# Head of a fused normalisation, attention and gated-MLP kernel: statistics and roots by two tiles, first product in column halves, first down weights split earlier

## The chip, the cores and the metric

The kernel runs on one core of a Trainium2 chip. The metric is the device time of one execution in microseconds. An execution of the kernel before takes 474.47 us (median of 3 runs, 474.45 to 474.83).

## What is computed

The input x has 2048 tokens of 512 features, in fp32. It is normalised over its features; the result feeds an attention over the 32 heads of each token by itself (query 16 by 32, key and value 16 by 8, each used for four heads) and a gated MLP with 1792 inner features. The MLP's result goes through a SiLU and gates the attention's result, and x is added.

```python
x = L0_attn_x                                    # (1, 2048, 512)
xn = _layernorm(x, axis=-1)
# attention of xn: q, k, v = xn @ W + b; scores over the 16 x 16 of one token
scores = jnp.einsum('bsdh,bseh->bsde', q, k) / np.float32(np.sqrt(D))
attn = jax.nn.softmax(scores, axis=-1)
out = jnp.einsum('bsde,bseh->bsdh', attn, v)
# MLP of xn
var = jnp.mean(jnp.square(x), axis=-1, keepdims=True)
nx = x * jax.lax.rsqrt(var + RMS_EPS) * ln_w
g = jnp.einsum('bsh,ih->bsi', nx, gate_w)
u = jnp.einsum('bsh,ih->bsi', nx, up_w)
return jnp.einsum('bsi,hi->bsh', jax.nn.silu(g) * u, down_w)
# end
g = _silu(_L0_ffn_ref(xn, ...))
x = x + s * g
```

## The kernel before

**Tiles.** A tile is 128 tokens by 512 features; four tiles (J) make a block of 512 tokens (TB), two blocks a pair (JJ = 8 tiles), and there are two pairs. Block 0 of the first pair is tiles 0 to 3, block 1 is tiles 4 to 7. The 1792 inner features are 14 groups (NI) of 128. Each operand of TensorE is kept as a high part (rounded to the matmul's format) and a low part (the rest), and each product is three matmuls: high by high, low weights by high data, high weights by low data. From group 1 on the gate and up products of two blocks are done by a scheme of seven products instead of eight (m1 to m7); group 0 is "plain": gate and up of block 0, then of block 1.

**Order.** Nothing is scheduled by the machine. Each engine has one queue written out by hand, and semaphores tie them. Five queues matter in the head, the first 28 us:

- SP issues the loads, in this order: x tiles 0 to 3, lnw, gate 0, the two halves of wq, up 0, wk, wv, x tile 4, the three biases, x tiles 5 to 7, gate 1, up 1 and two down weights.
- DVE (VectorE) takes the statistics of a tile (stats_tile, L1075), its mean and variance (variance, L1059 and L1061), and for tiles 0 to 3 normalises it (normalise_tile, L1070). Then it makes the low parts of the first weights (first_lo, L1166), four tiles of z_lo (L1119), the rest of first_lo, the statistics of tiles 4 to 7 with the low parts of the qkv weights (lo_qkv, L1289) behind those of tile 4, and takes the qkv products out of PSUM (qkv_take, L1192).
- POOL (GpSimd) takes the roots: scale_tile (L477, and for tiles 4 to 7 the shift, L482) and rms_of (L486, L487, L489), which qkv_take needs. It sums the queries' weights over four heads (sum_queries, L511 and L514) and the query bias (L526, L529), and later makes low parts: wd_lo_part (L504) and h_lo_part (L498).
- ACT (ScalarE) makes high parts: first_hi (L807), z_hi_tile (L840), hi_qkv (L953), hi_wd (L828), h_hi_part (L916). It normalises tiles 4 to 7 (z_tile, L833) and copies transposed tiles to SBUF (z_raw_tile, L844).
- TensorE (PE) runs 32 warm-up transposes, transposes tiles 0 to 3 (L727), and then first_gate0 (L583, L586, L589), first_up0 (L599, L600, L603), qkv_product(0) (L714, L715, L718), tile 4's transposes, qkv_product(1), the transposes of tiles 5 and 6, qkv_product(2), tile 7, qkv_product(3), gate1 and up1 of group 0 (L572 to L574), four more qkv products, and from there the groups 1 to 13 (L553, L555, L556 and the down products, L687 to L689).

A tile of block 1 is transposed into the PSUM bank (y_ps) of the tile four before it, once z_raw_tile has copied that one. The order of ACT in the middle of the head is z_tile(4), z_tile(5), z_hi_tile(4), z_tile(6), z_tile(7), z_raw_tile(4), z_hi_tile(5), z_hi_tile(6). In the code J is 4, so L833 for tile 5 is z_tile(J + 1).

## Time and profile before

| | |
|---|---|
| median of 3 runs | 474.47 us |
| the profiled execution's own time | 474.35 us |
| its span, first to last instruction | 472.6 us |
| around the span | 1.75 us |
| TensorE busy | 466.3 us, 99% |
| DVE busy | 412.7 us, 87% |
| ACT busy | 244.2 us, 52% |
| POOL busy | 123.1 us, 26% |
| DMA | 105.70 MB, mean 224 GB/s |

A busy share counts the time in which an engine executes; a row of the timeline gives the start, the duration, the engine, the line and the tiles of one instruction, or of several merged ones (xN). Starts are microseconds from the span's start. PEld is TensorE's loading of weights, which overlaps its matmuls (PE). SPq is the queue of SP as it issues DMAs.

### The profile page before, as it was taken

Reading aid. Unit: us, or ns where it says so; the run is one execution under the profiler, and the core shown is the slowest. Engines: PE = TensorE matmul, PEld = TensorE weight load, DVE = VectorE, ACT = ScalarE, POOL = GpSimd, SP = SyncE. Lnnn points to the kernel's source line nnn. Section 1 sums busy time; section 2 is a strip of 40 time slices with the busy share of each in tenths; the row PEclk is TensorE's granted clock in tenths of the full one; section 3 lists DMA queues with packets and bytes.
Section 4 is the critical chain, followed back from the end, with each engine's and each line's share of the span. In section 5 each row is a group of like instructions: output and inputs, shape, how many; then the busy total and the mean of one; then the engine's idle time right before and its main releaser. Section 6 shows DMA issues by size and latency. Waiting matters only on the chain.

```text
span 472.6 us, 6217 instructions
## 1 busy us (share of the span) xinstructions
PE 466.3 (99%) x2122; PEld 391.0 (83%) x2122; DVE 412.7 (87%) x561; ACT 244.2 (52%) x417; POOL 123.1 (26%) x106
## 2 busy tenths in 40 slices
PE   7999999999999999999999999999999999999997
PEld 7898888888888888888888888888888888888886
DVE  6889778987898898889989898999998888888994
ACT  4785656658588888654122545225225335358102
POOL 5740312126222122233443101000011111126920
PEclk9999999999999999999999999999999999999999
DMA  8605996579779996573474649546556655514772
GB/s 269 252 2 225 345 380 262 234 259 273 205 248 301 298 360 255 188 268 133 135 235 162 218 187 371 202 184 223 222 201 223 223 200 200 201 44 135 276 259 89
DMA packets 44623, 105.70 MB, mean 224 GB/s; under 512 B 20272, under 2 KB 21808, under 8 KB 41264
## 3 DMA queue, kind: packets, MB, share of 16 engines
q1 hardware_dynamic: 44592, 105.31, 63.3%
q8 instruction: 17, 0.28, 0.2%
q14 instruction: 14, 0.11, 0.1%
HBM read 69.90 MB, written 35.40 MB: 223 GB/s over the span
## 4 chain that ended last, share of the span: by engine, by line
PE 95%; DVE 2%; DMA 1%; ACT 1%; SPq 0%; POOL 0%; issue 0%
PE gu_ps L553 18%; PE gu_ps L555 18%; PE gu_ps L556 18%; PE y_ps L687 8%; PE y_ps L688 8%; PE y_ps L689 8%; PE gu_ps L688 3%; PE gu_ps L687 3%; PE gu_ps L689 3%; PE gu_ps L718 2%; PE gu_ps L715 2%; PE gu_ps L714 2%; DMA xz<-x 1%; DVE w_ops L1166 1%; PE y_ps L727 0%; DVE stats L1075 0%
## 5 line engine op out<-in xcount | busy, mean ns | idle before, releaser
L553 PE MATMUL gu_ps<-z_hi,w_ops 128*128 128x512 f32 x378 | 147.2, 390 | 0.1
L556 PE MATMUL gu_ps<-z_hi,w_ops 128*128 128x512 f32 x378 | 147.1, 389 | 0.0
L555 PE MATMUL gu_ps<-z_lo,w_ops 128*128 128x512 f32 x378 | 147.1, 389 | 0.0
L498 POOL TENSOR_TENSOR h_lo<-h,h_hi 128x512 fp32r<-128x512 f32 x28 | 37.4, 1335 | 226.8 <-ACT h_hi L916 226.6
L553 PEld LDWEIGHTS gu_ps<-z_hi,w_ops 128*128 128x128 f32 x378 | 71.0, 188 | 15.5 <-issue 0.4
L556 PEld LDWEIGHTS gu_ps<-z_hi,w_ops 128*128 128x128 f32 x378 | 70.9, 188 | 14.8
L555 PEld LDWEIGHTS gu_ps<-z_lo,w_ops 128*128 128x128 f32 x378 | 70.9, 188 | 14.5
L687 PE MATMUL y_ps<-wd_ops,h_hi 128*128 128x512 f32 x168 | 65.6, 390 | 0.0
L689 PE MATMUL y_ps<-wd_ops,h_lo 128*128 128x512 f32 x168 | 65.5, 390 | 0.0
L688 PE MATMUL y_ps<-wd_ops,h_hi 128*128 128x512 f32 x168 | 65.5, 390 | 0.0
L916 ACT ACTIVATE h_hi<-h 128x512 fp32r<-128x512 f32 x28 | 17.6, 630 | 58.9 <-DVE h L1208 58.9
L1250 DVE TENSOR_TENSOR prod<-scores,qkv 128x1024 f32<-128x1024 f32 x32 | 43.2, 1351 | 0.8
L1232 DVE TENSOR_TENSOR prod<-qkv 128x1024 f32<-128x1024 f32 x32 | 41.8, 1305 | 0.6
L1253 DVE TENSOR_REDUCE attn<-prod 128x64 f32<-128x1024 f32 x32 | 38.9, 1217 | 0.8
L1235 DVE TENSOR_REDUCE scores<-prod 128x128 f32<-128x1024 f32 x32 | 38.9, 1215 | 0.6
L687 PEld LDWEIGHTS y_ps<-wd_ops,h_hi 128*128 128x128 f32 x168 | 31.5, 188 | 6.9 <-POOL h_lo L498 0.6
L689 PEld LDWEIGHTS y_ps<-wd_ops,h_lo 128*128 128x128 f32 x168 | 31.5, 188 | 6.6
L688 PEld LDWEIGHTS y_ps<-wd_ops,h_hi 128*128 128x128 f32 x168 | 31.5, 188 | 6.3
L891 ACT ACTIVATE u<-gu_ps 128x512 f32<-128x512 f32 x27 | 16.1, 598 | 38.9 <-PE gu_ps L556 38.9
L504 POOL TENSOR_TENSOR wd_ops<-raw,wd_ops 128x512 fp32r<-128x512 f32 x14 | 19.7, 1405 | 57.4 <-ACT wd_ops L828 27.6
L1220 DVE TENSOR_TENSOR h_kept<-u 128x512 f32<-128x512 f32 x27 | 22.3, 828 | 12.8 <-ACT u L904 10.0
L498 POOL TENSOR_TENSOR h_lo<-h_kept,h_hi 128x512 fp32r<-128x512 f32 x15 | 23.3, 1556 | 35.4 <-ACT h_hi L916 34.4
(139 smaller groups left out, 753.0 us busy)
## 6 DMA issues: line engine op xcount, KB each, us to landing
w_kept<-w_ops SPq DMA_DIRECT2D x13, 1792.0 KB, 6.2
w_ops<-w_kept SPq DMA_DIRECT2D x13, 1792.0 KB, 7.6
wd_ops<-wd_kept SPq DMA_DIRECT2D x35, 512.0 KB, 4.0
raw<-gate_up SPq DMA_DIRECT2D x30, 256.0 KB, 3.9
wd_kept<-wd_ops SPq DMA_DIRECT2D x14, 512.0 KB, 7.8
xz<-x SPq DMA_DIRECT2D x16, 256.0 KB, 5.3
raw<-down SPq DMA_DIRECT2D x14, 256.0 KB, 8.5
w_ops<-wd_kept SPq DMA_DIRECT2D x7, 512.0 KB, 7.5
```

The costliest lines, as they stand in the source:

```text
L498: pool.tensor_tensor(lo, src, hi.bitcast(F32), ALU.subtract).then_inc(h_lo_done, 1)
L553: pe.matmul(acc, w_h, z_hi[:, zi, c, :], start=start and c == 0, stop=False, skip_group_check=True)
L555: pe.matmul(acc, w_h, z_lo[:, zi, c, :], start=False, stop=False, skip_group_check=True)
L556: end = pe.matmul(acc, w_l, z_hi[:, zi, c, :], start=False, stop=c == 1, skip_group_check=True)
L687: pe.matmul(acc, hi, wd[:, 0, t], start=n == 0, stop=False, skip_group_check=part)
L688: pe.matmul(acc, hi, wd[:, 1, t], start=False, stop=False, skip_group_check=part)
L689: pe.matmul(acc, lo, wd[:, 0, t], start=False, stop=n == NI - 1, skip_group_check=part)\
L1220: dve.tensor_tensor(h_kept[:, g % NI, :], u2[:], up, ALU.mult).then_inc(h1_done, 1)
L1232: return dve.tensor_tensor(pr, q[:, d:d + HALF, :].unsqueeze(2).to_broadcast([P, HALF, D, HKV]), k.unsqueeze(1).to_broadcast([P, HALF, D, ...
L1235: return dve.tensor_reduce(s[:, d:d + HALF, :], pr, X, ALU.add)
L1250: return dve.tensor_tensor(pr, e[:, d:d + HALF, :].unsqueeze(2).to_broadcast([P, HALF, HKV, D]), v.unsqueeze(1).to_broadcast([P, HALF, HKV ...
L1253: return dve.tensor_reduce(o[:, d:d + HALF, :], pr, X, ALU.add)
```

## The change

- lnw is loaded by ACT's queue instead of SP's, ahead of its table load. On SP's queue up 0 goes ahead of wq, and x tiles 5 and 6 ahead of the biases.
- DVE takes the statistics of tiles 0 and 1, then the variance of both in one instruction, then the same for 2 and 3, and only then normalises the four tiles. POOL takes the roots of two tiles in one instruction (scale_two). x_variance(0) stands behind first_lo(0).
- On POOL rms_of for tiles 0 to 3 goes from ahead of sum_queries to behind scale_tile(J), which is tile 4's root and shift.
- TensorE's first_gate0 and first_up0 become first_products: the gate's products of high parts and those with z_lo are made in two halves of 256 columns, each waiting for its own two tiles, and a part of the up products stands between the two halves with z_lo. qkv_product(0) waits for wqkv by halves.
- On ACT first_hi(1) goes ahead of the first two z_raw_tile, and hi_wd(0) from behind the last z_raw_tile to between z_hi_tile(J + 2) and z_raw_tile(J + 1).

```diff
@@ -400,19 +400,18 @@
                         sp.dma_start(out_tiles[J * f + j, :, t], fin_x[f][:, j, t]).then_inc(fin_stored, 16)
 
             load_x(0, range(0, J))
-            sp.dma_start(lnw_sb[:], lnw).then_inc(lnw_in, 16)
             load_gate(0)
+            load_up(0)
             for a in (0, 2):
                 sp.dma_start(wq_raw[:, a:a + 2, :], wq.rearrange("(k p) n -> p k n", p=P)[:, a:a + 2, :])\
                   .then_inc(wq_in[a // 2], 16)
-            load_up(0)
             sp.dma_start(wqkv_raw[:, :, DG:2 * DG], wk.rearrange("(k p) n -> p k n", p=P)).then_inc(wkv_in, 16)
             sp.dma_start(wqkv_raw[:, :, 2 * DG:], wv.rearrange("(k p) n -> p k n", p=P)).then_inc(wkv_in, 16)
-            load_x(0, (J,))
+            load_x(0, range(J, JJ - 1))
             sp.dma_start(bq_raw, bq.partition_broadcast(P)).then_inc(bias_in, 16)
             sp.dma_start(bias[:, DG:2 * DG], bk.partition_broadcast(P)).then_inc(bias_in, 16)
             sp.dma_start(bias[:, 2 * DG:], bv.partition_broadcast(P)).then_inc(bias_in, 16)
-            load_x(0, range(J + 1, JJ))
+            load_x(0, (JJ - 1,))
             load_gate(1)
             load_up(1)
             load_down(0)
@@ -471,15 +470,18 @@
                                pattern=[[-1, P]], channel_multiplier=1).then_inc(const_done, 1)
             pool.wait_ge(const_done, 3)
 
+            def scale_two(j):
+                pool.wait_ge(var_done, j + 2)
+                t = slice(j, j + 2)
+                pool.tensor_tensor(z_scale[:, t], z_var[:, t], minus_half[:, t], ALU.pow).then_inc(z_scale_done, 2)
+
             def scale_tile(j):
-                pool.wait_ge(var_done, j + 1 + (j >= J))
-                t = slice(j, j + 1)
+                pool.wait_ge(var_done, j + 2)
+                t, m = slice(j, j + 1), slice(j - J, j - J + 1)
                 pool.tensor_tensor(z_scale[:, t], z_var[:, t], minus_half[:, t], ALU.pow).then_inc(z_scale_done, 1)
-                if j >= J:
-                    m = slice(j - J, j - J + 1)
-                    pool.wait_ge(z_scale_done, j + 1)
-                    pool.wait_ge(mean_done, j - J + 1)
-                    pool.tensor_tensor(z_shift[:, m], minus_mean[:, m], z_scale[:, t], ALU.mult).then_inc(z_shift_done, 1)
+                pool.wait_ge(z_scale_done, j + 1)
+                pool.wait_ge(mean_done, j - J + 1)
+                pool.tensor_tensor(z_shift[:, m], minus_mean[:, m], z_scale[:, t], ALU.mult).then_inc(z_shift_done, 1)
 
             def rms_of(first, count, step, tile):
                 t = slice(first, first + count)
@@ -514,13 +516,13 @@
                 pool.tensor_tensor(wqkv_raw[:, k, 0:DG], quads[:, :, :, 0, 0], quads[:, :, :, 1, 0], ALU.add)\
                     .then_inc(wqkv_summed, 1)
 
-            for j in range(J):
-                scale_tile(j)
-            pool.wait_ge(var_done, J + 1)
-            rms_of(0, J, 1, 0)
+            scale_two(0)
+            scale_two(2)
             sum_queries(0)
             sum_queries(1)
             scale_tile(J)
+            pool.wait_ge(var_done, J + 1)
+            rms_of(0, J, 1, 0)
             pool.wait_ge(bias_in, 48)
             bias_quads = bq_raw.rearrange("p (n s r) -> p n s r", s=2, r=2)
             pool.tensor_tensor(bias_quads[:, :, :, 0], bias_quads[:, :, :, 0], bias_quads[:, :, :, 1], ALU.add)\
@@ -574,34 +576,42 @@
                         end = pe.matmul(acc, w_l, z_hi[:, zi, c, :], start=False, stop=last)
                 return end
 
-            def first_gate0():
-                acc = gu_ps[:, GATE_BANK, :]
-                chunks = [(wi, zi, c) for wi, zi in ((WA11, ZB11), (WA12, ZB21)) for c in range(2)]
+            def first_products():
+
+                gate, up = gu_ps[:, GATE_BANK, :], gu_ps[:, UP_BANK, :]
+                gates = [(wi, zi, c) for wi, zi in ((WA11, ZB11), (WA12, ZB21)) for c in range(2)]
+                ups = [(wi, zi, c) for wi, zi in ((WA21, ZB11), (WA22, ZB21)) for c in range(2)]
+                halves = slice(0, TB // 2), slice(TB // 2, TB)
+
+                def w_part(s, wi, c):
+                    return w_ops[:, 0, s, wi, c * P:(c + 1) * P]
+
                 pe.wait_ge(w_hi_a, 1)
-                pe.wait_ge(z_hi_done, J)
-                for n, (wi, zi, c) in enumerate(chunks):
-                    pe.matmul(acc, w_ops[:, 0, 0, wi, c * P:(c + 1) * P], z_hi[:, zi, c, :], start=n == 0, stop=False)
+                for a, t in enumerate(halves):
+                    pe.wait_ge(z_hi_done, 2 * a + 2)
+                    for n, (wi, zi, c) in enumerate(gates):
+                        pe.matmul(gate[:, t], w_part(0, wi, c), z_hi[:, zi, c, t], start=a + n == 0, stop=False,
+                                  skip_group_check=True)
                 pe.wait_ge(w_lo_a, 1)
-                for wi, zi, c in chunks:
-                    pe.matmul(acc, w_ops[:, 0, 1, wi, c * P:(c + 1) * P], z_hi[:, zi, c, :], start=False, stop=False)
+                for wi, zi, c in gates:
+                    pe.matmul(gate, w_part(1, wi, c), z_hi[:, zi, c, :], start=False, stop=False, skip_group_check=True)
+                pe.wait_ge(z_lo_done, 2)
+                for wi, zi, c in gates:
+                    pe.matmul(gate[:, halves[0]], w_part(0, wi, c), z_lo[:, zi, c, halves[0]], start=False, stop=False,
+                              skip_group_check=True)
+                pe.wait_ge(w_hi_a, 2)
+                for n, (wi, zi, c) in enumerate(ups):
+                    pe.matmul(up, w_part(0, wi, c), z_hi[:, zi, c, :], start=n == 0, stop=False)
                 pe.wait_ge(z_lo_done, J)
-                for n, (wi, zi, c) in enumerate(chunks):
-                    end = pe.matmul(acc, w_ops[:, 0, 0, wi, c * P:(c + 1) * P], z_lo[:, zi, c, :], start=False,
-                                    stop=n == 3)
+                for n, (wi, zi, c) in enumerate(gates):
+                    end = pe.matmul(gate[:, halves[1]], w_part(0, wi, c), z_lo[:, zi, c, halves[1]], start=False,
+                                    stop=n == 3, skip_group_check=True)
                 end.then_inc(m2_done, 1)
-
-            def first_up0():
-                acc = gu_ps[:, UP_BANK, :]
-                chunks = [(wi, zi, c) for wi, zi in ((WA21, ZB11), (WA22, ZB21)) for c in range(2)]
-                pe.wait_ge(w_hi_a, 2)
-                for n, (wi, zi, c) in enumerate(chunks):
-                    w_h = w_ops[:, 0, 0, wi, c * P:(c + 1) * P]
-                    pe.matmul(acc, w_h, z_hi[:, zi, c, :], start=n == 0, stop=False)
-                    pe.matmul(acc, w_h, z_lo[:, zi, c, :], start=False, stop=False)
+                for wi, zi, c in ups:
+                    pe.matmul(up, w_part(0, wi, c), z_lo[:, zi, c, :], start=False, stop=False)
                 pe.wait_ge(w_lo_a, 2)
-                for n, (wi, zi, c) in enumerate(chunks):
-                    end = pe.matmul(acc, w_ops[:, 0, 1, wi, c * P:(c + 1) * P], z_hi[:, zi, c, :], start=False,
-                                    stop=n == 3)
+                for n, (wi, zi, c) in enumerate(ups):
+                    end = pe.matmul(up, w_part(1, wi, c), z_hi[:, zi, c, :], start=False, stop=n == 3)
                 end.then_inc(m4_done, 1)
 
             def gate1(g):
@@ -709,12 +719,14 @@
                 zi, t = 2 * (j // J), slice((j % J) * P, (j % J + 1) * P)
                 z_h = [z_hi[:, zi + k // 2, k % 2, t] for k in range(K)]
                 z_l = [z_lo[:, zi + k // 2, k % 2, t] for k in range(K)]
-                pe.wait_ge(wqkv_hi_done, 2)
                 for k in range(K):
+                    if index == 0:
+                        pe.wait_ge(wqkv_hi_done, k // 2 + 1)
                     pe.matmul(acc, z_h[k], wqkv_hi[:, k, :], start=k == 0, stop=False)
                     pe.matmul(acc, z_l[k], wqkv_hi[:, k, :], start=False, stop=False)
-                pe.wait_ge(wqkv_lo_done, 2)
                 for k in range(K):
+                    if index == 0:
+                        pe.wait_ge(wqkv_lo_done, k // 2 + 1)
                     end = pe.matmul(acc, z_h[k], wqkv_lo[:, k, :], start=False, stop=k == K - 1)
                 end.then_inc(qkv_done, 1)
 
@@ -736,8 +748,7 @@
                 pe.transpose(y_ps[:, 0, 0:P], ident[:], ident[:])
             for j in range(J):
                 transpose_tile(y_ps[:, j, :], j)
-            first_gate0()
-            first_up0()
+            first_products()
             qkv_product(0)
             second_tile(J)
             qkv_product(1)
@@ -944,6 +955,7 @@
                     acc = gu_ps[:, j, t] if f == 3 and n == 0 else y_ps[:, j, t]
                     act.activation(fin_y[:, j, t], acc, ACT.Silu).then_inc(y_done, 1)
 
+            act.dma_start(lnw_sb[:], lnw).then_inc(lnw_in, 16)
             load_silu()
             act.wait_ge(lnw_in, 16)
             def hi_qkv(half_of_k):
@@ -955,9 +967,9 @@
             first_hi(0)
             for j in range(J):
                 z_hi_tile(j)
+            first_hi(1)
             z_raw_tile(0)
             z_raw_tile(1)
-            first_hi(1)
             hi_qkv(0)
             hi_qkv(1)
             z_raw_tile(2)
@@ -971,11 +983,11 @@
             z_raw_tile(J)
             z_hi_tile(J + 1)
             z_hi_tile(J + 2)
+            hi_wd(0)
             z_raw_tile(J + 1)
             z_hi_tile(J + 3)
             z_raw_tile(J + 2)
             z_raw_tile(J + 3)
-            hi_wd(0)
             h_hi_part(0)
             scale(1)
             hi_a(1)
@@ -1054,9 +1066,16 @@
 
         @block.vector
         def _(dve):
-            def variance(j):
+            def aggregate(j):
                 dve.wait_ge(bn_done, j + 1)
                 dve.bn_aggr(mean_var[:, j, :], stats[:, j, :]).then_inc(stats_done, 1)
+
+            def two_variances(j):
+                dve.wait_ge(stats_done, j + 2)
+                dve.tensor_scalar(z_var[:, j:j + 2], mean_var[:, j:j + 2, 1], 1.0 + EPS, EPS * EPS,
+                                  ALU.mult, ALU.add).then_inc(var_done, 2)
+
+            def variance(j):
                 dve.wait_ge(stats_done, j + 1)
                 dve.tensor_scalar(z_var[:, j:j + 1], mean_var[:, j, 1:2], 1.0 + EPS, EPS * EPS,
                                   ALU.mult, ALU.add).then_inc(var_done, 1)
@@ -1290,22 +1309,22 @@
                                   ALU.subtract).then_inc(wqkv_lo_done, 1)
 
             dve.memset(scratch[:, 0:1], 0.0).then_inc(table_loaded, 1)
+            for j in (0, 2):
+                stats_tile(j)
+                stats_tile(j + 1)
+                aggregate(j)
+                aggregate(j + 1)
+                two_variances(j)
             for j in range(J):
-                stats_tile(j)
-                if j:
-                    variance(j - 1)
-                if j > 1:
-                    normalise_tile(j - 2)
-            variance(J - 1)
-            normalise_tile(J - 2)
+                normalise_tile(j)
+            first_lo(0)
             x_variance(0)
-            normalise_tile(J - 1)
-            first_lo(0)
             for j in range(J):
                 z_lo_tile(j)
             first_lo(1)
             for j in range(J, JJ):
                 stats_tile(j)
+                aggregate(j)
                 variance(j)
                 mean_of(j)
                 if j == J:
```

## Rows read from the trace of the kernel before

**Rows 1.** Page, 40 slices of the span: granted clock of TensorE, tenths

```profile
PEclk9999999999999999999999999999999999999999
```

**Rows 2.** Waits of TensorE, whole span: us in total, times, longest

```profile
PE gu_ps L583 <- ACT z_hi L840: 0.8, 1, 0.8
```

**Rows 3.** Waits of TensorE's weight loads, 27 us to the end

```profile
PEld gu_ps L553 <- issue: 0.4, 1, 0.4
PEld gu_ps L553 <- ACT u L891: 0.3, 1, 0.3
```

**Rows 4.** Timeline, TensorE, 18 to 23 us: start, us, engine, line, operation

```profile
18.46 0.98 PE L718 MATMUL gu_ps<-wqkv_lo,z_hi 128*128 128x384 f32 x4
...
19.45 0.63 PE L727 MATMUL y_ps<-ident,xz 128*128 128x128 f32 x4
...
22.86 0.19 PEld L714 LDWEIGHTS gu_ps<-wqkv_hi,z_hi 128*128 128x128 f32 x1
```

**Rows 5.** Timeline, DVE, 9 to 19 us

```profile
9.00 0.56 DVE L1070 TENSOR_SCALAR xz<-xz,mean_var,z_scale 128x512 f32<-128x512 f32 x1
9.48 1.12 DVE L1166 SCALAR_TENSOR_TENSOR w_ops<-raw,lnw_sb,w_ops 128x128 fp32r<-128x128 f32 x4
10.53 2.47 DVE L1119 TENSOR_TENSOR z_lo<-y_ps,z_hi 128x512 fp32r<-128x512 f32 x4
...
13.64 1.97 DVE L1166 SCALAR_TENSOR_TENSOR w_ops<-raw,lnw_sb,w_ops 128x128 fp32r<-128x128 f32 x4 [0.64 <-ACT w_ops L807]
...
15.53 0.68 DVE L1075 BATCH_NORM_STATS2 stats<-xz 128x6 f32<-128x512 f32 x1
...
16.59 1.81 DVE L1289 TENSOR_TENSOR wqkv_lo<-qkv,wqkv_hi 128x768 fp32r<-128x768 f32 x2
```

**Rows 6.** Timeline, POOL, 11 to 25 us

```profile
11.44 1.04 POOL L511 TENSOR_TENSOR h_kept<-h_kept 128x512 f32<-128x512 f32 x1
...
14.29 0.64 POOL L514 TENSOR_TENSOR qkv<-h_kept 128x256 f32<-128x256 f32 x1
16.69 1.26 POOL L477 TENSOR_TENSOR z_scale<-z_var,minus_half 128x1 f32<-128x1 f32 x1 [1.76 <-DVE z_var L1061]
...
18.41 0.61 POOL L526 TENSOR_TENSOR h_kept<-h_kept 128x256 f32<-128x256 f32 x1
...
19.50 0.56 POOL L477 TENSOR_TENSOR z_scale<-z_var,minus_half 128x1 f32<-128x1 f32 x1
...
22.40 1.02 POOL L486 TENSOR_TENSOR x_rstd<-x_var,minus_half 128x4 f32<-128x4 f32 x1
...
24.47 0.20 POOL L489 TENSOR_TENSOR rms<-x_rstd,z_std 128x4 f32<-128x4 f32 x1
```

**Rows 7.** Timeline, ACT, z_tile of tiles 5 and 6, 20 to 22 us

```profile
20.36 0.82 ACT L833 ACTIVATE xz<-xz,z_shift,z_scale 128x512 f32<-128x512 f32 x1 [1.05 <-POOL z_shift L482]
...
21.56 0.80 ACT L833 ACTIVATE xz<-xz,z_shift,z_scale 128x512 f32<-128x512 f32 x1
```

**Rows 8.** Timeline, SP's issues of DMAs, 0 to 20 us

```profile
0.74 1.80 SPq L310 DMA_DIRECT2D xz<-x  x4
...
3.53 0.95 SPq L406 DMA_DIRECT2D h_kept<-wq  x2
...
6.41 1.77 SPq L310 DMA_DIRECT2D xz<-x  x1
```

**Rows 9.** DMA issues, 2.5 to 2.7 us (x tile 3): KB, us to landing

```profile
xz<-x SPq DMA_DIRECT2D x1, 256.0 KB, 3.9
```

**Rows 10.** DMA issues, 6.4 to 6.6 us (x tile 4)

```profile
xz<-x SPq DMA_DIRECT2D x1, 256.0 KB, 7.7
```

**Rows 11.** DMA issues, 3.5 to 3.6 us (first half of wq)

```profile
h_kept<-wq SPq DMA_DIRECT2D x1, 512.0 KB, 6.1
```

**Rows 12.** Timeline, DVE, t_add, 26 to 34 us

```profile
27.97 1.23 DVE L1142 TENSOR_TENSOR h_kept<-h_kept 128x1024 f32<-128x1024 f32 x1 [0.67 <-ACT h_kept L844]
...
29.64 4.04 DVE L1142 TENSOR_TENSOR h_kept<-h_kept 128x1024 f32<-128x1024 f32 x2
```

## The prediction

> **What bounds the kernel now.** The page comes first: TensorE is busy 99% of the span (the table above), and its granted clock is full in all 40 slices [rows 1]. So only its idle time is to be had. The waits say where that is: 0.8 us ahead of the first product [rows 2], and after 27 us only 0.4 and 0.3 us ahead of L553 among what this change can touch [rows 3]. Everything from there on is a dense stream of matmuls, so the end moves by what the head moves. The timeline of the head then shows who paces TensorE. At 19.45 it takes the transposes of tile 4, and at 22.86 it loads the first weights of qkv_product(2); in between it runs without a hole [rows 4]. I call 22.86 the mark: whatever moves it moves the end, less what later waits give back.
>
> **Backwards from the mark.** ACT normalises tile 6 from 21.56 to 22.36, 0.50 us ahead of the mark, and tile 5 from 20.36 [rows 7]. Tile 5 needed its root from POOL, at 19.50, which follows POOL's bias additions (18.41) without a hole; those follow tile 4's root and shift (16.69) [rows 6]. That needed DVE's statistics of tile 4 at 15.53, which stand right behind first_lo(1), 13.64 to 15.61 [rows 5]. So the head is one chain: DVE up to the statistics of tile 4 (call their start S, now 15.53), then POOL, then ACT, then TensorE.
>
> **The change, up to S.** lnw leaves SP's queue, so each later issue is up to 0.48 us earlier. ACT issues it before its table load, and ACT is idle until gate lands, so that costs nothing there. What does not move is the load of the DMA engines. x tile 3 is the last of four issues in 1.80 us, so issued at 2.1, and lands 3.9 us later, at 6.0 [rows 8, 9]. x tile 4 lands at 6.41 + 7.7 = 14.1 with the same bytes ahead of it as before [rows 8, 10]; I take 14.0 as a floor for S. The first half of wq lands at 3.53 + 6.1 = 9.6 [rows 8, 11]; the 1.5 MB from there to tile 4's landing took 4.5 us, 0.75 us for 256 KB, and now up is ahead of it, so 10.4 (9.6 if the order counts for little).
> Statistics in twos: the variances are known some 1.1 us after the last statistics start (15.53 to 16.59 for tile 4 [rows 5]), so from 6.0 at 7.1. A root of one column takes 0.56 us and of four 1.02 [rows 6], so two take about 0.7, up to 1.26, what the single root at 16.69 took beside DVE. The normalisation of tile 2 then starts at 8.0 to 8.5 and that of tile 3 at 8.5 to 9.0, against 9.00 [rows 5]. Tile 0's normalisation comes later, but tiles 0 and 1 wait for nothing that ends last. Of what follows on DVE nothing is shorter: first_lo(0), the x variance and four z_lo come next: 9.00 to 12.93 now (four z_lo take 2.47 from 10.53, overlapping by 0.07), and the small x variance, which stood ahead of 9.00; 4.1 us with it [rows 5]. So first_lo(1) can start at 12.6 to 13.1. It used to wait for ACT until 13.64; ACT's first_hi(1) now stands before two z_raw and is through by then.
> first_lo(1) took 1.97 us beside POOL's sums of wq, against 1.05 for first_lo(0), 9.48 to 10.53. POOL's sums took 11.44 to 14.93, 3.49 us, and S came 0.60 us behind them [rows 5, 6]. Starting at 10.4 they end at 13.9, which puts S at 14.5; starting at 9.6, S is at its floor, 14.0. I take 14.3, a gain of 1.2 us up to here.
> What these rows show of DVE and POOL beside each other is what the Trainium skill has in "SBUF — State Buffer", section "Who interferes with whom": a DVE operation with two SBUF inputs shuts out a POOL operation that reads SBUF, and the other way round, for the whole instruction. By it z_lo, which reads PSUM, is free to run beside the sums, and S is POOL's end plus two pieces, as at 14.93. The page "DMA: Bandwidth & Descriptors", section "Issuing engines are not separate DMA queues", speaks against the first edit: the queues interleave on the same 16 engines, and a second issuer saves only issue time. The landings above are in line with it.
>
> **The change, behind S.** TensorE's halves move the same matmuls and columns earlier (qkv_product(0) can end near 17.7 instead of 19.15), as do the waits for halves of wqkv. But TensorE then stands before tile 4 and tile 5, which are POOL's and ACT's, so this is worth nothing at the mark; its cover is about 2 us.
> The step that decides is the moved rms_of. Its three operations ran before the sums, ahead of S. Now they stand behind tile 4's root, in front of the bias additions, and the roots of tiles 5 to 7 are queued behind them. Their like at 22.40 takes 22.40 to 24.67, 2.27 us [rows 6]. From S to POOL's free moment after tile 4 is 18.41 - 15.53 = 2.88 us (DVE's lo_qkv at 16.59 holds it up as before), then 2.27, then the bias additions, 19.50 - 18.41 = 1.09: the root of tile 5 starts at S + 6.24 instead of S + 3.97. Tile 5's variance is ready long before. From that root to ACT's tile 5 is 0.86 us, from there to its tile 6 1.20, then 0.80 and 0.50 to the mark [rows 6, 7]: 9.60 us from S. With S = 14.3 the mark is at 23.90, 1.04 us later than 22.86. So the head gains 1.2 us and POOL takes 2.3 from it, as the transposes of tile 6 had no slack to speak of.
> The bias loads now land behind x tiles 5 and 6, but are wanted only at S + 5.15 = 19.5, and tile 7's x is wanted later still: nothing. qkv_take(0) waits for the same bias sums; it has 2 us until DVE's next z_lo: nothing.
>
> **What comes back.** The down weights' high part of ACT (0.6 us) is moved between two z_hi, where ACT waited for DVE anyway. POOL's wd_lo then leaves the stretch in which DVE's two t_add took 4.04 us beside POOL's wd_lo and h_lo, where one took 1.23 just before [rows 12]. From there DVE is dense to qkv_take(6), whose end released L553 at 41.7. If DVE comes 0.7 us sooner against TensorE, the 0.2 us that TensorE idled there is gone, and perhaps 0.1 of the later 0.3 [rows 3]. These bound it: 0 to 0.35; I take 0.25.
>
> **Sum.** +1.04 - 0.25 = +0.8 us. The profiled execution takes 474.35 us (472.6 and 1.75 around the span), so 475.15; it lies 0.12 under the median of 474.47, so the forecast is 475.3. Ends: S = 14.0 with all given back, +0.74 - 0.35 = +0.4; S = 14.5 and nothing given back, +1.24.
>
> **The rivals.** *Slower beyond doubt:* POOL's sums wait for wq longer than I allow and drag on first_lo(1). It decides from S = 14.45 on (14.45 + 9.60 - 22.86 - 0.25 = 0.94); at S = 14.8 the time is +1.5 less 0.25, 475.7, and without anything given back 476.0. For it speaks that up is now ahead of wq, and that DVE had 0.9 us of disturbance in before; against it that x tile 4's bytes are unchanged.
> *Faster:* the moved rms_of is covered. If bias additions and rms_of fitted ahead of tile 5's variance, or spans of POOL's roots in the rows are overstated, the mark is S + 7.33 as before, 21.63, and the time 474.47 - 1.23 - 0.1 = 473.1. Against it stand three rows of one operation back to back and an ordered queue; for it only that POOL's spans are rough.
> *The edit does not do what it says:* the twos and halves bring nothing because the roots in twos eat it. S stays over 15 and the time is over 476.3; it needs two roots to take over 2 us, which no row shows.
> *The clock:* TensorE takes tile 4 at S + 3.9 as before and is through with qkv_product(1) some 2.6 us later (22.86, less 0.85 for eight transposes, less 19.45), while ACT's tile 5 ends at S + 6.24 + 0.86 + 0.82 = S + 7.9: it idles about 1.5 us there and 0.7 before tile 6. The longest hole of before, 1 us ahead of L583, left the granted clock full [rows 1, 2]. If it fell from 2.4 to 1.2 GHz, the 12 matmuls of qkv_product(2) would take twice three times the 0.7 that the four at 18.46 take up to the next issue [rows 4], 2.1 us more: over 477.
>
> **How the numbers follow.** A measurement of this kernel tells 0.2%, 0.95 us, from no change: 473.5 to 475.4 is "same". Forecast case 0.47; slower beyond 475.4 by S or by nothing given back 0.35; faster 0.13; the edit without effect at its front 0.02; the clock 0.03. That gives faster 0.13, same 0.47, slower 0.40. The range leaves out the faster case and the last two, and reaches from a little under S at its floor, 474.1, to S of 14.8 without give-back, 476.1.
>
> **What would show it.** In the profile after: statistics of tile 4 start at 14.0 to 14.6; POOL's two roots of four columns and their product stand behind tile 4's shift, and tile 5's root starts near S + 6.2 with DVE's variance of tile 5 done 2 us before; TensorE waits some 1.5 us for ACT's tile 5 and again for tile 6; qkv_product(2) starts near 23.9; L553's wait near 42 is gone. The prediction is wrong if POOL's rms_of takes under 1 us there, if TensorE reaches tile 6 later than ACT, or if S is over 15.

## The result, and the profile after

The change makes the kernel slower: 478.00 us (median of 5, 477.0 to 478.96) against 474.47, a ratio of 1.0073 with a 95% interval of 1.0053 to 1.0092. That is +3.5 us where +0.8 was forecast, and above the range's end of 476.1. The profiled execution took 478.96 us, with a span of 477.2.

The chain of the prediction can be read off again; S is the start of tile 4's statistics on DVE, and the mark is the load of the first weights of qkv_product(2). First DVE, from the roots of the first tiles to the low parts of wqkv (timeline of the changed kernel, DVE, start and duration in us):

```profile
6.67 0.69 DVE L1094 BATCH_NORM_STATS2 stats<-xz 128x6 f32<-128x512 f32 x1 [0.60 <-DMA xz<-x]
...
7.76 2.14 DVE L1089 TENSOR_SCALAR xz<-xz,mean_var,z_scale 128x512 f32<-128x512 f32 x4
9.82 3.61 DVE L1185 SCALAR_TENSOR_TENSOR w_ops<-raw,lnw_sb,w_ops 128x128 fp32r<-128x128 f32 x4
...
13.43 2.47 DVE L1138 TENSOR_TENSOR z_lo<-y_ps,z_hi 128x512 fp32r<-128x512 f32 x4
15.82 1.13 DVE L1185 SCALAR_TENSOR_TENSOR w_ops<-raw,lnw_sb,w_ops 128x128 fp32r<-128x128 f32 x4
16.87 0.69 DVE L1094 BATCH_NORM_STATS2 stats<-xz 128x6 f32<-128x512 f32 x1
```

The second row of w_ops is as it should be, 1.13 us for four; the first, the same four operations, takes 3.61. In the kernel before it was the other way: 1.12 for the first and 1.97 for the second [rows 5]. S (last row) is 16.87 instead of 15.53; 14.3 was forecast. Now POOL:

```profile
8.00 0.87 POOL L476 TENSOR_TENSOR z_scale<-z_var,minus_half 128x2 f32<-128x2 f32 x1 [1.64 <-DVE z_var L1075]
9.65 1.16 POOL L513 TENSOR_TENSOR h_kept<-h_kept 128x512 f32<-128x512 f32 x1 [0.78 <-DMA h_kept<-wq]
10.88 0.65 POOL L516 TENSOR_TENSOR qkv<-h_kept 128x256 f32<-128x256 f32 x1
11.48 1.08 POOL L513 TENSOR_TENSOR h_kept<-h_kept 128x512 f32<-128x512 f32 x1
12.65 0.64 POOL L516 TENSOR_TENSOR qkv<-h_kept 128x256 f32<-128x256 f32 x1
18.04 1.26 POOL L481 TENSOR_TENSOR z_scale<-z_var,minus_half 128x1 f32<-128x1 f32 x1 [4.75 <-DVE z_var L1080]
19.38 0.43 POOL L484 TENSOR_TENSOR z_shift<-minus_mean,z_scale 128x1 f32<-128x1 f32 x1
19.76 1.01 POOL L488 TENSOR_TENSOR x_rstd<-x_var,minus_half 128x4 f32<-128x4 f32 x1
20.74 1.00 POOL L489 TENSOR_TENSOR z_std<-z_var,half 128x4 f32<-128x4 f32 x1
...
23.05 0.56 POOL L481 TENSOR_TENSOR z_scale<-z_var,minus_half 128x1 f32<-128x1 f32 x1
```

The four sums of wq run from 9.65 to 13.29, exactly beside the slow first_lo(0), which ends at 13.43. Then POOL stands idle for 4.75 us, and the two roots of four columns that it could have taken there come behind tile 4's root. Tile 5's root starts at 23.05, S + 6.18; S + 6.24 was forecast, and it was S + 3.97 before [rows 6]. Last TensorE, first its waits, then the granted clock in stretches of 2 us (us of the stretch; busy us of PE, PEld, DVE, ACT, POOL with instructions; clock, DMA share, GB/s):

```profile
PE y_ps L739 <- ACT xz L844: 1.9, 2, 1.3
PE y_ps L748 <- POOL ident L469: 1.5, 1, 1.5
PE gu_ps L597 <- DVE w_ops L1185: 1.4, 1, 1.4
```

```profile
24.00:26.00 2.00, 0.63 (x4) 0.42 (x4) 0.77 (x2) 2.00 (x4) 1.84 (x5) 1.00 0.03 8
26.00:28.00 2.00, 1.95 (x8) 1.98 (x9) 0.84 (x2) 2.00 (x5) 1.57 (x3) 0.54 0.00 0
28.00:30.00 2.00, 2.00 (x8) 2.00 (x8) 1.49 (x3) 1.07 (x3) 1.29 (x1) 0.60 0.01 4
30.00:32.00 2.00, 2.00 (x14) 1.97 (x14) 1.17 (x2) 1.09 (x2) 0.00 (x0) 1.00 0.00 0
```

```profile
26.62 0.34 PEld L725 LDWEIGHTS gu_ps<-wqkv_hi,z_hi 128*128 128x128 f32 x1
...
32.55 0.19 PEld L574 LDWEIGHTS gu_ps<-z_hi,w_ops 128*128 128x128 f32 x1
```

TensorE waits 1.3 and 0.6 us for tiles 5 and 6, and behind these holes its granted clock is at the lower of its two levels (1.2 of 2.4 GHz) for most of 26 to 30 us: 0.54 and 0.60 as means of 2 us. The first weights of qkv_product(2), the mark, are loaded at 26.62 instead of 22.86, +3.76: 1.34 from S, 2.21 from POOL's roots, and 0.2 of the transposes of tile 6 at the low clock. From the mark to the first weights of gate1 it takes 5.93 us; the kernel before took 4.56 (27.42 - 22.86), so the low clock costs 1.4 us more there. That makes +5.13 at gate1, of which 0.5 come back behind it: the span is 4.6 longer.

The executions differ with the clock. Two of the five had a mean granted clock of 0.996 and took 478.96 and 478.82 us; the other three, at 0.999 or 1.0, took 477.0, 477.5 and 478.0. Only the first of them has a trace.

### The profile page after: what moved, and what is told of

Same layout as the page of the kernel before. It is cut to its first block, busy times and chain, and to the rows that moved or that the text cites. A ratio compares the mean times of both kernels' runs of the same rounds, so it can differ in the third digit from the quotient of the medians.

```text
span 477.2 us, 6229 instructions
## 1 busy us (share of the span) xinstructions
PE 467.4 (98%) x2130; PEld 392.8 (82%) x2130; DVE 413.8 (87%) x559; ACT 243.9 (51%) x417; POOL 121.0 (25%) x104
## 4 chain that ended last, share of the span: by engine, by line
PE 94%; DVE 2%; POOL 1%; DMA 1%; ACT 1%; SPq 0%; issue 0%; POOLq 0%; DVEq 0%
PE gu_ps L558 18%; PE gu_ps L557 18%; PE gu_ps L555 18%; PE y_ps L697 8%; PE y_ps L699 8%; PE y_ps L698 8%; PE gu_ps L698 3%; PE gu_ps L697 3%; PE gu_ps L699 3%; PE gu_ps L726 2%; PE gu_ps L725 2%; PE gu_ps L730 2%; DVE w_ops L1185 1%; DMA xz<-x 1%; DVE z_lo L1138 1%; PE gu_ps L575 0%
```

## The experiments

Theory: three costs, one behind the other. (1) POOL's sums of wq, moved earlier, run beside first_lo(0) and make it slow (the expectations call this the port theory; the runs can show the slowing, not that a port is its reason); (2) the moved rms_of delays tiles 5 to 7 by its 2.2 us (queue theory); (3) the holes that this opens in TensorE make the clock fall in some executions (clock theory). Rivals: S is late because x tile 3 lands late (6.6 instead of 6.0) or because of the statistics in twos; POOL's roots are covered; the clock has another cause. Each ratio is to the kernel before, timed on the same chip (its medians there are 474.9 to 475.1).

### The three costs, each taken away

**e1_rms_early**: rms_of back in its place, which also keeps POOL from the sums for 2.2 us; x_variance(0), which it needs, goes ahead of first_lo(0).

```diff
             scale_two(2)
+            pool.wait_ge(var_done, J + 1)
+            rms_of(0, J, 1, 0)
             sum_queries(0)
             sum_queries(1)
             scale_tile(J)
-            pool.wait_ge(var_done, J + 1)
-            rms_of(0, J, 1, 0)
...
-            first_lo(0)
             x_variance(0)
+            first_lo(0)
```

> The changed kernel with rms_of of tiles 0 to 3 back ahead of the sums of wq on POOL (and x_variance(0) ahead of first_lo(0), which it needs). Queue theory: the root of tile 5 follows tile 4's statistics (S) by 4.0 us again instead of 6.2, so 2.2 us come back; and rms_of keeps the sums off POOL until about 11.2, when first_lo(0) is through in 1.05 us instead of 3.61, so S falls from 16.9 to about 15.3. Mark (first weights of qkv_product(2)) near 22.7, no hole of 1.3 us ahead of tile 5, clock full: 474.0 to 474.5 us. Rival, that the later landing of x tile 3 and the statistics in twos make S late by themselves: S stays over 16 and the time is 475 to 476.

Measured: 474.16 us (11 executions, 473.81 to 475.09), ratio 0.9985 (0.9976 to 0.9993), faster than the kernel before. Timeline of DVE in e1:

```profile
7.38 0.69 DVE L1094 BATCH_NORM_STATS2 stats<-xz 128x6 f32<-128x512 f32 x1 [1.20 <-DMA xz<-x]
...
10.60 1.13 DVE L1185 SCALAR_TENSOR_TENSOR w_ops<-raw,lnw_sb,w_ops 128x128 fp32r<-128x128 f32 x4
...
14.04 2.75 DVE L1185 SCALAR_TENSOR_TENSOR w_ops<-raw,lnw_sb,w_ops 128x128 fp32r<-128x128 f32 x4
16.72 0.68 DVE L1094 BATCH_NORM_STATS2 stats<-xz 128x6 f32<-128x512 f32 x1
```

first_lo(0) is back at 1.13 us, and the sums, now 13.01 to 16.65, sit on first_lo(1) instead. Tile 5's root is at 20.69, S + 3.97. S at 16.72 is later than I expected, as x tile 3 landed at 7.3 in this execution, and that is paid for in full: with 475.09 us it is the slowest of the eleven. The profiled execution of e5 (below; the same kernel but for its loads) has S 0.83 sooner, at 15.89, and takes 474.23 us, 0.86 less. So the median, 474.16 us, is that of the theory with an S near 15.8 (an estimate from these two), and the rival (475 to 476) is out for the median only; the profiled execution is a case of it.

**e2_sums_late**: only the overlap with first_lo(0) taken away.

```diff
+            pool.wait_ge(w_lo_a, 1)
             sum_queries(0)
```

> The changed kernel with the sums of wq on POOL held until first_lo(0) is done, rms_of left behind tile 4's root. Port theory: first_lo(0) takes 1.05 us instead of 3.61, z_lo starts near 11.0 instead of 13.43, first_lo(1) is stretched by the sums instead, S is 15.0 to 15.3 instead of 16.87; rms_of still costs its 2.2 us behind it, the mark is S + 9.6 = 24.7, and the time 475.8 to 476.3, if the clock holds. Rival, that the sums only move their contention: S stays at 16.5 or more and the time at 477.5.

Measured: first_lo(0) 1.13 us, S at 15.46, tile 5's root at 21.61 (S + 6.15). The median is 477.23 us (9 executions), ratio 1.0038 (1.0024 to 1.0052), but that is two groups: three executions with a clock of 0.999 or 1.0 at 475.38, 475.43 and 475.95, and six at 0.996 at 476.7 to 477.9. The forecast for a full clock was 475.8 to 476.3; of the first three one lies in it and two 0.4 us under it. S rules out the rival (16.5 or more). The changed kernel's executions without the fall lie near 477.5, so the overlap costs about 1.9 us; it is 2.4 if each kernel is taken against its own timing of the kernel before, and 1.7 by the rows (first_lo(0) 3.61 less 1.13, first_lo(1) 1.88 less 1.13). The other group is put down to cost (3), 1.3 to 2 us, by its mean clock alone: the profiled execution is the one of 475.95 us, whose clock stayed full.

**e3_busy** and **e9_late_busy**: the holes of TensorE filled, in the changed kernel and in e2. The result of these transposes is read by nobody.

```diff
             qkv_product(1)
+            pe.wait_ge(z_raw_done, 2)
+            for n in range(12):
+                pe.transpose(y_ps[:, 1, 0:P], ident[:], ident[:])
             second_tile(J + 1)
+            pe.wait_ge(z_raw_done, 3)
+            for n in range(6):
+                pe.transpose(y_ps[:, 2, 0:P], ident[:], ident[:])
             second_tile(J + 2)
```

> The changed kernel with 12 transposes of the identity, whose result nobody reads, on TensorE ahead of tile 5's transposes and 6 ahead of tile 6's, in its holes of 1.3 and 0.6 us. Clock theory: the fall to 0.54 granted at 26 to 30 us in the profiled execution is due to those holes and costs about 1.5 us where it happens; with the holes filled the granted clock is full in all runs, the runs lie within 0.3 us of each other, at 477.0 to 477.5. Rival, that the clock follows something else: the spread of 477.0 to 479.0 stays and some runs show a clock under 1.

> e2_sums_late with TensorE's two holes filled as in e3_busy (12 and 6 transposes nobody reads). In e2_sums_late 6 of 9 executions had a mean granted clock of 0.996 and took 476.7 to 477.9 us, the other three 0.999 or 1.0 and 475.4 to 476.0. Clock theory: with the holes filled no execution has 0.996, and all lie at 475.4 to 476.2, a ratio to before near 1.002. Rival, that the fall has another cause: a third or more of the executions are still at 0.996 and 477.

Measured: e3 477.59 us (5 executions, 477.0 to 478.34), ratio 1.0054 (1.0041 to 1.0067). The stretches of the low clock read, in e3:

```profile
24.00:26.00 2.00, 1.97 (x18) 1.76 (x17) 0.62 (x2) 1.95 (x4) 1.84 (x6) 1.00 0.00 0
26.00:28.00 2.00, 2.00 (x15) 1.89 (x14) 0.84 (x3) 2.00 (x5) 1.71 (x3) 1.00 0.00 0
28.00:30.00 2.00, 2.00 (x15) 1.97 (x14) 2.00 (x4) 1.83 (x5) 1.19 (x1) 1.00 0.01 4
```

No execution has 0.996, but five are few, they spread over 1.3 us, more than I expected, and their median is not below the changed kernel's by anything clear. e9: 475.61 us (11 executions), ratio 1.0020 (1.0010 to 1.0029), and none at 0.996 where e2 had six of nine. The eighteen unread transposes go with a median 1.6 us lower, but by the ratios it is 0.9 us and the intervals overlap; the two also ran on different chips. So that filling the holes keeps the clock up is well supported (none of 16 executions at 0.996 in e3 and e9), and what it gains in time less so. Eight of e9's executions lie at 474.8 to 475.8; three at 476.6 to 477.0, with 0.998 or 0.999, are more than the theory has, and what sets them apart was not found.

**e12_change_again**: the changed kernel beside others on one chip.

> The changed kernel itself once more, beside the others on one chip. Theory: two groups of executions, those at a mean granted clock of 0.996 near 4.4 us above the kernel before and those at 0.999 or 1.0 some 2.5 to 3.5 us above it; first_lo(0) takes over 2.5 us and S is 16.5 or more. Rival, that the first result was the chip's: under 2 us above.

Measured: 477.73 us (6 executions, 476.33 to 479.02), ratio 1.0058 (1.0041 to 1.0075). So the loss is not a matter of the chip. The two groups did not come out as expected: one execution is at 0.996, 478.86 us (3.8 above the kernel before, for 4.4), and the five at 0.999 or 1.0 are 1.3 to 4.0 above it, two of them under the 2 us that the rival names. In the profiled execution x tile 3 lands at 7.4, S is 17.58 and first_lo(0) takes 2.78. TensorE has the same two holes ahead of tiles 5 and 6, 1.35 and 0.56 us, and the clock stays full there, as in the profiles of e2 and e4: the holes do not make it fall each time. That execution is the slowest, 479.02, with a clock of 0.999. Its late S is one part; the other is far behind the head (waits of e12, PE and PEld):

```profile
PE gu_ps L555 <- ACT gu_ps L890: 0.6, 1, 0.6
PEld gu_ps L555 <- issue: 1.0, 1, 1.0
```

This is a single wait at 171 us, for ACT, which had itself waited 1.24 us for a load of gate and up weights at 164.8. It costs 0.9 us and has nothing to do with the change; e8's profiled execution has one of 1.1 us at 168 us.

### The same in the kernel before

**e4_before_rms_late** and **e15_before_rms_late_free**: nothing of the change but rms_of behind tile 4's root; in e4 the sums also wait for first_lo(0), in e15 they don't.

```diff
             for j in range(J):
                 scale_tile(j)
-            pool.wait_ge(var_done, J + 1)
-            rms_of(0, J, 1, 0)
+            pool.wait_ge(w_lo_a, 1)
             sum_queries(0)
             sum_queries(1)
             scale_tile(J)
+            pool.wait_ge(var_done, J + 1)
+            rms_of(0, J, 1, 0)
```

In e15 the line with w_lo_a is left out.

> The kernel before with one edit: rms_of of tiles 0 to 3 behind tile 4's root on POOL, as in the change; and so that the sums of wq don't slide onto first_lo(0), they wait for it. Queue theory: S is 14.9 to 15.5 (the sums end 0.8 us sooner), the root of tile 5 starts at S + 6.2, the mark is S + 9.6 = 24.5 to 25.1 and the time 476.1 to 476.7. Rival, that POOL's roots are covered: the mark is S + 7.3 and the time 474.0.

> The kernel before with rms_of behind tile 4's root and nothing to hold the sums of wq back (e4 held them until first_lo(0) was done and took 1.6 us more than before). Port theory: the sums start when wq lands, near 9.7 to 10.8, and stretch first_lo(0) or, where wq lands later, not; S is later than in e4 by 0 to 2.5 us, which the landing of wq decides, and the time 0.5 to 2 us above e4's: a ratio of 1.0045 to 1.008. Rival, that the sums hurt only with the statistics in twos: the ratio is e4's, 1.0035 to 1.004.

Measured: e4 476.56 us (7 executions), ratio 1.0040 (1.0027 to 1.0054). S is 15.21, the root of tile 5 at 21.39, S + 6.18. Five executions with a full clock take 476.2 to 476.6, two at 0.995 and 0.996 take 477.7 and 478.2. e15 478.44 us (5 executions), ratio 1.0068 (1.0054 to 1.0081). DVE and POOL in e15:

```profile
10.74 2.77 DVE L1166 SCALAR_TENSOR_TENSOR w_ops<-raw,lnw_sb,w_ops 128x128 fp32r<-128x128 f32 x4
...
17.59 0.68 DVE L1075 BATCH_NORM_STATS2 stats<-xz 128x6 f32<-128x512 f32 x1
```

```profile
9.49 1.04 POOL L511 TENSOR_TENSOR h_kept<-h_kept 128x512 f32<-128x512 f32 x1
...
12.45 0.65 POOL L514 TENSOR_TENSOR qkv<-h_kept 128x256 f32<-128x256 f32 x1
```

One moved step of POOL, in a kernel with neither twos nor halves, has the whole loss of the change. The sums follow the roots at once and stretch DVE's last normalisation (9.59, 1.22 us) and first_lo(0). Not all of S is theirs: tile 3's statistics start at 7.12 in this execution, 0.6 us later than in the kernel before. Two of e15's executions are at 0.996 and 0.991 (478.44 and 478.71 us), but two of those at 1.0 took 477.88 and 478.72: here a low mean clock goes with no clear loss. In the profiled one the clock is down to 0.71 and 0.50 at 12 to 16 us, in the first products and not behind the holes of tiles 5 and 6, and the mark is at S + 9.53 and gate1 4.56 us behind it, as without a fall.

Set side by side, the profiled executions show what a late S and the moved steps are worth. Each entry is the time of the profiled execution less its S:

| rms_of | hi_wd(0) | time less S, us |
|---|---|---|
| early | behind the last z_raw | before 458.8 |
| early | moved | e1, e5, e6, e7, e10, e13, e14 458.3 to 458.4; e11 458.6 |
| late | behind the last z_raw | e4 461.0, e15 460.9 |
| late | moved | e2, e3, e9 460.5 to 460.6; e12 461.4; changed kernel 462.1 |

S runs from 14.49 to 17.59 in these, so each microsecond of S is a microsecond of the time. The late rms_of costs 2.1 us in both kernels, the moved hi_wd(0) gives 0.4, e12's wait at 171 us is its 0.9, and the low clock of the changed kernel is its 1.6. e8 (459.9) has the wait at 168 us in it.

### What the rest of the change is worth

**e8_hiwd_back** (e1 with hi_wd(0) back behind the last z_raw) and **e13_before_hiwd** (the kernel before with hi_wd(0) moved as in the change, the diff shown; e8 is its reverse):

```diff
             z_hi_tile(J + 2)
+            hi_wd(0)
             z_raw_tile(J + 1)
...
             z_raw_tile(J + 3)
-            hi_wd(0)
             h_hi_part(0)
```

> As e1_rms_early, with the down weights' high part back behind the last z_raw on ACT. Give-back theory: POOL's wd_lo is again beside DVE's two t_add, which take 4 us instead of some 3.2, TensorE waits 0.2 us ahead of L555 at 42 us, and the time is 0.2 to 0.3 us longer than e1_rms_early, a ratio to before of 0.9990. Rival, that the step is worth nothing or costs: the ratio is 0.9985 or less.

> The kernel before with one edit: the down weights' high part between z_hi of tiles 6 and 7. If the give-back of 0.7 us that e8_hiwd_back shows is this step's alone, the two t_add take 3.05 us instead of 4.04, TensorE's waits ahead of L553 (0.4 and 0.3 us) are gone, and the ratio to before is 0.9983 to 0.9987. Rival, that it needs the rest of the change: the ratio is 0.9995 or more.

Measured: e8 474.85 us, ratio 1.0002 (0.9993 to 1.0011): without the step e1's gain is gone, 0.8 us by the ratios where 0.2 to 0.3 was expected. e13 474.45 us, ratio 0.9988 (0.9979 to 0.9998), 0.55 us on its own. The traces give 0.4 to 0.5 us; what e8 shows above that may be waits like the one at 168 us, which was not tried. t_add in e8 and in e13:

```profile
29.82 4.04 DVE L1161 TENSOR_TENSOR h_kept<-h_kept 128x1024 f32<-128x1024 f32 x2
```

```profile
30.06 3.05 DVE L1142 TENSOR_TENSOR h_kept<-h_kept 128x1024 f32<-128x1024 f32 x2
```

**e5_loads_before** and **e6_lnw_sp**, both on e1: all loads as in the kernel before, and lnw alone.

```diff
             load_x(0, range(0, J))
+            sp.dma_start(lnw_sb[:], lnw).then_inc(lnw_in, 16)
             load_gate(0)
...
-            act.dma_start(lnw_sb[:], lnw).then_inc(lnw_in, 16)
```

> As e1_rms_early (rms_of early), and all loads in the order of the kernel before, lnw on SP's queue again. x tile 3, whose landing took 4.5 to 5.2 us with the new order and 3.6 to 3.9 with the old, lands at about 6.0 instead of 6.7 to 7.4, so the last normalisation and all behind it come 0.7 us sooner and S is near 15.7 instead of 16.7. But up 0 lands behind wq, so ACT's first_hi(1) starts near 12.8 as in the kernel before. Load theory: 0.5 to 0.8 us faster than e1_rms_early, a ratio to before of 0.997. Rival, that landings vary from run to run and the order does not matter: the ratio stays 0.9985.

> As e1_rms_early, with only lnw back on SP's queue, behind the four x tiles; up 0 stays ahead of wq. If lnw's 128 small packets on ACT's queue, beside x, are what delays x tile 3, it lands in 3.6 to 3.9 us and the ratio is 0.997; if it is gate and up issued right behind x, it still takes 4.5 us or more and the ratio is that of e1_rms_early, 0.9985.

Measured: 474.19 us each, ratios 0.9986 (0.9978 to 0.9995) and 0.9987 (0.9978 to 0.9996), the same as e1: the order of the loads moves the median by nothing that can be measured, and the 0.5 us and more that I had expected of e5 did not come. x tile 3 took 4.2 and 4.1 us to land. Over all profiled executions it took 3.6 to 4.3 us in the six kernels with lnw on SP's queue, and 3.8 to 5.6, median 4.8, in the eleven with lnw on ACT's. So the second queue probably does delay x, with one execution of each kernel to go by; how was not tried further.

**e7_xvar_first**: e1 with the x variance ahead of the normalisations, so that rms_of and then the sums start earlier.

```diff
+            x_variance(0)
             for j in range(J):
                 normalise_tile(j)
-            x_variance(0)
             first_lo(0)
```

> As e1_rms_early, with x_variance(0) ahead of the four normalisations. POOL's rms_of then starts at the end of the second root of two, near 9.2 instead of 10.8, and the sums of wq 1.6 us sooner, which takes 1 to 1.5 us of their overlap off first_lo(1). Port theory: first_lo(1) takes under 2 us instead of 2.75, S is 0.8 us sooner than in e1_rms_early and the ratio to before is 0.997. Rival, that the sums then sit on first_lo(0) as in the change: first_lo(0) takes over 2 us and the ratio is 0.9985 or more.

Measured: 473.82 us (8 executions, 472.87 to 474.15), ratio 0.9976 (0.9965 to 0.9986), the lowest ratio of all, though its interval overlaps e1's (e1, e5, e6, e10, e11, e13 and e14 are faster than the kernel before too). On the same chip it is 0.4 us under e5 and e6. POOL and DVE in e7:

```profile
8.18 1.10 POOL L488 TENSOR_TENSOR x_rstd<-x_var,minus_half 128x4 f32<-128x4 f32 x1
...
10.39 1.04 POOL L513 TENSOR_TENSOR h_kept<-h_kept 128x512 f32<-128x512 f32 x1
```

```profile
9.16 1.13 DVE L1185 SCALAR_TENSOR_TENSOR w_ops<-raw,lnw_sb,w_ops 128x128 fp32r<-128x128 f32 x4
10.21 2.47 DVE L1138 TENSOR_TENSOR z_lo<-y_ps,z_hi 128x512 fp32r<-128x512 f32 x4
12.61 1.96 DVE L1185 SCALAR_TENSOR_TENSOR w_ops<-raw,lnw_sb,w_ops 128x128 fp32r<-128x128 f32 x4
14.49 0.68 DVE L1094 BATCH_NORM_STATS2 stats<-xz 128x6 f32<-128x512 f32 x1
```

rms_of, whose operands are four columns, runs beside first_lo(0) and does it no harm, and fills POOL's time until first_lo(0) is done (10.29); the sums then fall mostly beside z_lo. S is 14.49, 2.2 us sooner than in e1, but not all of that is the edit's: x tile 3 landed 1.4 us sooner in this execution, which is the fastest of the eight.

**e10_no_halves, e11_no_twos, e14_no_twos_no_halves**: e7 with the first products in whole width (first_gate0 and first_up0 of the kernel before), with statistics and roots tile by tile, and with both.

```diff
-            first_products()
+            first_gate0()
+            first_up0()
```

```diff
-            scale_two(0)
-            scale_two(2)
+            for j in range(J):
+                scale_one(j)
...
-            for j in (0, 2):
+            for j in range(J):
                 stats_tile(j)
-                stats_tile(j + 1)
-                aggregate(j)
-                aggregate(j + 1)
-                two_variances(j)
+                if j:
+                    aggregate(j - 1)
+                    variance(j - 1)
+                if j > 1:
+                    normalise_tile(j - 2)
```

> e7_xvar_first with the first products as in the kernel before (whole width, gate and then up, waiting for all four tiles). If the halves only fill TensorE's time ahead of tile 4's transposes, which ACT sets, the time is that of e7_xvar_first, a ratio to before of 0.9975 to 0.998. If they are worth something, TensorE comes late to tile 4 and the ratio is 0.9985 or more.

> e7_xvar_first with statistics, variances and roots tile by tile as in the kernel before. The x variance, and rms_of behind it, are then ready near 8.9 instead of 7.1, the last normalisation starts at 9.0 instead of 8.7, and POOL's sums end 1 us later, near 14.9, which stretches first_lo(1): S near 15.4 instead of 14.5 and a ratio to before of 0.999 to 1.000. Rival, that the twos gain nothing: the ratio stays 0.9976.

> e7_xvar_first with neither the twos nor the halves. e10 and e11 took them out one at a time and lost nothing that can be measured. If they are worth nothing together either, the ratio to before is 0.9975 to 0.9982; if each stood in for the other, it is 0.999 or more.

Measured: ratios 0.9977 (0.9968 to 0.9985), 0.9980 (0.9971 to 0.9989) and 0.9979 (0.9970 to 0.9988), 473.68, 474.00 and 474.00 us. Neither is worth anything that can be measured, alone or together. For the twos I had expected a loss of 0.7 us and more; that was wrong. e14 is the kernel before with the new loads, first_hi(1) and hi_wd(0) earlier, qkv's waits by halves and x_variance(0) one normalisation sooner, and it too is 1.0 us under the kernel before.

## Why the prediction was wrong

Step by step, in its own order.

- *What bounds the kernel, and the chain behind S.* Right. The mark was put at S + 9.60 and is at S + 9.75, of which 0.2 is the low clock; the root of tile 5 is at S + 6.18 for 6.24. The seven kernels with the moved rms_of have S + 6.15 to S + 6.18, the ten with it in its place S + 3.96 or 3.97.
- *S: the step that failed.* "Of what follows on DVE nothing is shorter" was taken to mean that nothing is longer either, and 4.1 us were carried over from [rows 5] for tile 3's normalisation, first_lo(0), the x variance and z_lo. Without the normalisation that is 3.6; it took 6.0 (9.82 to 15.82), of which first_lo(0) is 3.61 instead of 1.05. S is 16.87 for 14.3, and over 15, which the prediction had named as a sign of being wrong. The working had both numbers that show why: the sums could start at 9.6, and first_lo(0) starts half a microsecond behind a normalisation put at 8.5 to 9.0. It looked at the sums only where they had stood before, beside first_lo(1), and counted their end instead of laying the whole of 9.6 to 13.3 beside DVE's queue. It also preferred 10.4 for the landing of wq because up 0 goes ahead of it; wq landed at 9.5, and for 9.6 the prediction has S sooner, at 14.0, where it is in fact later. The rule of the Trainium skill ("SBUF — State Buffer", section "Who interferes with whom") was applied to one of the two steps of DVE that read two SBUF operands, first_lo(1), and not to first_lo(0), where the trace agrees with it: 3.61 us for 1.12. The rival for a late S was there with a chance of 0.35, but with the wrong mechanism (sums that come late); they came early.
- *x tile 3.* It landed at 6.6 for 6.0. Tile 3's normalisation ended 0.3 us later than in the kernel before, instead of up to 0.5 sooner, while first_lo(0) alone is 2.5 us longer. e5 and e6 show that the order of the loads is worth no measurable time in the median; a single late landing is, as e1's profiled execution shows.
- *The clock.* Named as a rival with a chance of 0.03 and a price of 2.1 us; it costs 1.6 in the trace. It fell in 2 of 5 executions here and in 6 of 9 of e2. The chance was taken from one hole, 0.8 us by [rows 2] and called 1 us, that had left the clock full [rows 1]. The changed kernel has two holes close together ahead of tiles 5 and 6, of 1.34 and 0.56 us, and one more of 1.4 us inside the first products; e2 and e4 lack that one and have low means too.
- *What comes back.* 0.25 us, between 0 and 0.35. e8 and e13 measure 0.8 and 0.55, the traces 0.4 to 0.5. The mechanism was right (4.04 to 3.05 us for the two t_add), the size was not: I counted TensorE's waits ahead of L553 in part only.
- *Halves, twos, order of the loads.* The halves were put at nothing: right (e10, e14). The twos were given up to 0.5 us of S and measure none (e11, e14). The order of the loads was given 0.8 us on wq's landing, which did not come, and moves the median by nothing (e5, e6).

The sum with the measured terms, for an execution without the fall of the clock: 1.34 for S, 2.21 for the roots, less the 0.5 that comes back, +3.05 us on 474.47, 477.5; with the fall (1.4 and 0.2 us) 479.1. The executions are at 477.0 to 478.0 and at 478.8 to 479.0. Against the forecast, the profiled span is 3.8 us too long (+4.6 for +0.8): 2.6 of it are S, 1.5 the clock, and what comes back is 0.25 the other way. Two of the prediction's own sums are loose besides: by its terms an S of 15 gives 476.0 to 476.2, not over 476.3, and its lowest case, +0.4, is 474.9, 0.8 above the low end of its range.

## What to carry to other kernels

When a step is moved out of an in-order queue, the steps behind it move up: lay their new times beside the queue of the engine that they slow down, over their whole length, and not beside what they stood next to before. Look for the idle time that the move leaves behind; here POOL waited 4.75 us for tile 4's variance and then, behind it, did 2.2 us of work whose input had been there since 13.5. A hole in a dense TensorE stream can cost its own length and then, in some executions, some 1.5 us of half clock; in e9 transposes that nobody reads cost nothing (the time less S is e2's) and no execution had the fall. And the profiled execution is one of several: read its own time and its S before its rows are taken for the median's.

## What was not expected of the hardware

- POOL's root of four columns (1.0 us) ran beside DVE's first_lo(0) without slowing it (1.13 us in e7, 1.12 before [rows 5]), where the sums of 512 and 256 columns stretched it to 2.77 to 3.61. The sums themselves lost little, 3.64 us for 3.49. The Trainium skill ("SBUF — State Buffer", section "Who interferes with whom") has a DVE instruction with two SBUF inputs contend with any POOL instruction that reads SBUF, by an exclusive lock; e7's rows show no such lock for the small operands.
- A mean granted clock of 0.996 or less came in 3 of 11 executions of the changed kernel (e12 with it), 6 of 9 of e2, 2 of 7 of e4 and 2 of 5 of e15, all with holes ahead of tiles 5 and 6 (1.3 and 0.6 us; 0.9 and 0.6 in e15's trace), and in none of 16 of e3 and e9, with the holes filled. The kernel before, timed beside them, has it in 2 of 101. The mean does not say where the clock fell: it was at 26 to 30 us in the trace of the changed kernel, and at 12 to 16 us in that of e15.
- The landing of one 256 KB tile of x, the fourth DMA of the kernel, took from 3.6 to 5.6 us over the profiled executions.
